# ScalarE's Silu in place of Sigmoid and a VectorE multiply in the attention of a decoder layer

## The reference

```python
qkv = silu(einsum('bnf,of->bno', x, w_qkv))      # 16 heads, 128 wide
q, k, v = split(qkv)
qk = einsum('bhmd,bhnd->bhmn', q, k) * decay      # causal, decays with the distance
out = einsum('bhmn,bhne->bhme', qk, v)            # the block form of the reference sums to this
out = norm_w * (out * rsqrt(mean(out * out) + 1e-6))
gate = sigmoid(einsum('bnf,of->bno', x, w_gate))
result = einsum('bno,fo->bnf', gate * out, w_out)
```

## Time and profile before

| | |
|---|---|
| median of 3 runs | 2632.61 us (2632.53 to 2634.94) |
| the profiled execution, its own time | 2630.53 us |
| its span, first to last instruction | 2628.8 us |
| mean granted clock of TensorE | 0.993 of full speed |
| busy: TensorE, VectorE, ScalarE, GpSimd | 98%, 81%, 42%, 26% of the span |
| ACT_TABLE_LOAD on ScalarE | 92 in the program |

### The profile page before, as it was taken

The page is one execution under the profiler, slowest core; times in us unless marked ns, Lnnn a source line. Parts: engine busy times, 40 slices in busy tenths (PEclk is TensorE's granted clock), DMA queues, the critical chain, the costliest instruction groups (busy, mean ns, idle before and its releaser), DMA issues.

```text
span 2628.8 us, 37692 instructions
## 1 busy us (share of the span) xinstructions
PE 2577.9 (98%) x12735; PEld 2102.3 (80%) x12735; DVE 2130.2 (81%) x4130; ACT 1100.7 (42%) x1862; POOL 690.5 (26%) x1030
## 2 busy tenths in 40 slices
PE   9999999999999999999999999999989999999995
PEld 7888888888888888888888888888877676767762
DVE  8888888887778888777888888777747888888887
ACT  4433333433335444333534443343324555555553
POOL 2111211311122231111223211022223444444444
PEclk9999999999999999999999999999999999999998
DMA  5555455444347654444665544363566555556632
GB/s 217 215 209 189 146 187 192 159 141 129 133 154 235 187 162 160 133 143 139 197 209 187 165 144 129 136 249 144 192 224 181 159 156 167 152 162 168 164 109 56
DMA packets 244943, 439.05 MB, mean 167 GB/s; under 512 B 100240, under 2 KB 135952, under 8 KB 236048
## 3 DMA queue, kind: packets, MB, share of 16 engines
q1 hardware_dynamic: 161056, 407.90, 46.1%
q10 hardware_dynamic: 81360, 20.07, 4.3%
q0 software_dynamic: 2336, 8.65, 1.6%
HBM read 286.35 MB, written 130.17 MB: 158 GB/s over the span
## 4 chain that ended last, share of the span: by engine, by line
PE 93%; DVE 4%; DMA 2%; issue 1%; ACT 1%; POOL 0%; SPq 0%; ACTq 0%; DVEq 0%; POOLq 0%
PE bank L834 39%; PE bank L1529 13%; PE bank L815 13%; PE bank L950 9%; PE bank L904 9%; PE bank L1573 6%; PE bank L1583 3%; PE bank L1550 1%; DMA attention_shared<-attention_x_in 1%; PE bank L1539 1%; DVE attention_stats L1007 0%; DMA finish_qT<-finish_q 0%; PE bank L842 0%; DMA finish_tT<-down_named 0%; PE bank L1561 0%
## 5 line engine op out<-in xcount | busy, mean ns | idle before, releaser
L834 PE MATMUL bank<-attention_xT,attention_w_hi 128*128 128x512 f32 x3064 | 948.4, 391 | 0.0
L834 PEld LDWEIGHTS bank<-attention_xT,attention_w_hi 128*128 128x128 f32 x3064 | 571.3, 188 | 114.5
L834 PE MATMUL bank<-attention_xT,attention_w_lo 128*128 128x512 f32 x1532 | 597.2, 390 | 0.0
L608 POOL TENSOR_TENSOR attention_sq_sum<-attention_sq_sum,attention_sq 128x512 f32<-128x512 f32 x120 | 188.3, 1569 | 966.9 <-ACT attention_sq L777 966.9
L834 PEld LDWEIGHTS bank<-attention_xT,attention_w_lo 128*128 128x128 f32 x1532 | 287.9, 188 | 59.6
L815 PE MATMUL bank<-attention_w_hi,attention_xT 128*128 128x512 f32 x1024 | 325.9, 400 | 9.6 <-DVE attention_sig_v L984 9.4
L734 ACT CAST attention_sh<-attention_sf 128x384 fp32r<-128x384 f32 (+1 forms) x384 | 186.0, 548 | 283.9 <-DVE attention_sf L1133 283.8
L1529 PE MATMUL bank<-finish_w_out_hi,finish_og 128*128 128x512 f32 x824 | 282.8, 408 | 0.2
L1143 DVE TENSOR_TENSOR attention_sl<-attention_sf,attention_sh 128x384 fp32r<-128x384 f32 (+1 forms) x384 | 227.8, 649 | 0.0
L815 PEld LDWEIGHTS bank<-attention_w_hi,attention_xT 128*128 128x128 f32 x1024 | 184.5, 190 | 42.9 <-issue 11.0
L1175 DVE SCALAR_TENSOR_TENSOR attention_og<-bank,attention_nw,attention_gate 128x512 f32<-128x512 f32 x128 | 96.0, 750 | 132.6 <-PE bank L950 119.1
(11 more groups left out here) (225 smaller groups left out, 4921.7 us busy)
## 6 DMA issues: line engine op xcount, KB each, us to landing
attention_xT<-normed_turned SPq DMA_DIRECT2D x62, 2048.0 KB, 8.6
gated_heads<-attention_og_out SPq DMA_DIRECT2D x64, 1024.0 KB, 7.7
finish_og<-gated_heads SPq DMA_DIRECT2D x103, 512.0 KB, 3.9
values<-attention_held SPq DMA_DIRECT2D x128, 256.0 KB, 2.8
attention_vh<-values SPq DMA_DIRECT2D x32, 512.0 KB, 8.1
attention_vl<-values SPq DMA_DIRECT2D x32, 512.0 KB, 9.4
finish_og_last<-gated_heads SPq DMA_DIRECT2D x25, 512.0 KB, 4.0
normed_turned<-attention_shared SPq DMA_DIRECT2D x24, 512.0 KB, 4.1
```

Of the source, the lines that this page charges most:

```text
L608: g.tensor_tensor(sq_sum[:, col_b], sq_sum[:, col_b], sq[:, :], ALU.add).then_inc(s_acc, 1)
L834: mm = pe.matmul(dst[:, :], part[a][w][:, k, col:col + P], xT[i][:, b, k, :], start=(k == 0 and s == 0), stop=(k == KD - 1 and s == 2))
```

## The change

ScalarE writes Silu instead of Sigmoid for queries, keys and values, into buffers with new names. VectorE's multiply by the bank is gone in all three (3 x 128 instructions), so its cast waits for ScalarE directly. The semaphores of steps count one less a round. TensorE's wait before a block of values is now for ScalarE's Silu of the block before, not for VectorE's multiply; so is the wait before the fourth transposition of x. The instruction that has the Sigmoid table loaded ahead of time (L706) now does so for Silu. The gate stays a Sigmoid.

```diff
-            nc.scalar.activation(sig_q[:, :], Q_BANK[:, :], ACT.Sigmoid).then_inc(s_sigq, 1)
+            nc.scalar.activation(silu_q[:, :], Q_BANK[:, :], ACT.Silu).then_inc(s_siluq, 1)
...
-            nc.scalar.activation(sig_k[:, :], K_BANK[:, :], ACT.Sigmoid).then_inc(s_sigk, 1)
+            nc.scalar.activation(silu_k[:, :], K_BANK[:, :], ACT.Silu).then_inc(s_siluk, 1)
...
-            nc.scalar.activation(sig_v[:, :], v_bank(q)[:, :], ACT.Sigmoid).then_inc(s_sigv, 1)
+            nc.scalar.activation(silu_v[:, :], v_bank(q)[:, :], ACT.Silu).then_inc(s_siluv, 1)
...
-        nc.scalar.activation(warm[:, :], dist[:, 0:1], ACT.Sigmoid)
+        nc.scalar.activation(warm[:, :], dist[:, 0:1], ACT.Silu)
...
             if q > 1:
-                pe.wait_ge(s_vm, 2 * (q - 2) + 3 if q > 2 else 1)
+                pe.wait_ge(s_siluv, q if q > 2 else 1)
...
             if n in PREPARED and PREPARED[n] > 1:
-                pe.wait_ge(s_qm, 2 * n + 3)
+                pe.wait_ge(s_siluq, n + 2)
...
-        def silu_split(n, src, f, h, l, sigd, steps, lo):
+        def split(n, f, h, l, sigd, steps, lo):
 
             v_.wait_ge(sigd, n + 1)
-            v_.tensor_tensor(f[:, :], src[:, :], f[:, :], ALU.mult).then_inc(steps, 1)
-            v_.wait_ge(steps, 2 * n + 1)
             v_.tensor_copy(h, f[:, :]).then_inc(steps, 1)
-            v_.wait_ge(steps, 2 * n + 2)
+            v_.wait_ge(steps, n + 1)
             v_.tensor_tensor(l, f[:, :], h.bitcast(F32), ALU.subtract).then_inc(lo, 1)
...
-            v_.wait_ge(s_sigv, q + 1)
-            v_.tensor_tensor(sig_v[:, :], v_bank(q)[:, :], sig_v[:, :], ALU.mult).then_inc(s_vm, 1)
-            v_.wait_ge(s_vm, 2 * q + 1)
+            v_.wait_ge(s_siluv, q + 1)
```

More of the change, by code:

```diff
@@ L225, in attention @@
     og_out = sb("og_out", [P, KT, 2, 2, P])
-    sig_q, sig_k, sig_v = sb("sig_q", [P, S]), sb("sig_k", [P, S]), sb("sig_v", [P, S])
+    silu_q, silu_k, silu_v = sb("silu_q", [P, S]), sb("silu_k", [P, S]), sb("silu_v", [P, S])
     qh, ql = sb("qh", [P, S], F32R), sb("ql", [P, S], F32R)
@@ L717, in scalar @@
         values_hi(1)
-        sig_query(0)
-        sig_key(0)
+        silu_query(0)
+        silu_key(0)
         weights_hi(QK1_W, 0)
-        sig_values(0)
+        silu_values(0)
         weights_hi(G_W, 0)
-        sig_values(1)
+        silu_values(1)
         for n, v, p, b, j in slots():
@@ L745, in scalar @@
             if n < LAST:
-                sig_query(n + 1)
-                sig_key(n + 1)
+                silu_query(n + 1)
+                silu_key(n + 1)
             if b == B - 2 and j == 1 and p + 1 < NP:
@@ L974, in queries @@
                 v_.wait_ge(s_s, 3 * n)
-            silu_split(n, Q_BANK, sig_q, qh[:, :], ql[:, :], s_sigq, s_qm, s_ql)
+            split(n, silu_q, qh[:, :], ql[:, :], s_siluq, s_qm, s_ql)
         def keys(n):
-            silu_split(n, K_BANK, sig_k, kh[:, :], kl[:, :], s_sigk, s_km, s_kl)
+            split(n, silu_k, kh[:, :], kl[:, :], s_siluk, s_km, s_kl)
         def values(q):
             t, i, r = q % KT, q // KT % B % 2, q % 2
-            v_.wait_ge(s_sigv, q + 1)
-            v_.tensor_tensor(sig_v[:, :], v_bank(q)[:, :], sig_v[:, :], ALU.mult).then_inc(s_vm, 1)
-            v_.wait_ge(s_vm, 2 * q + 1)
+            v_.wait_ge(s_siluv, q + 1)
             if q > 1:
@@ L988, in values @@
             own, other = slice(0, 2 * P), slice(2 * P, 4 * P)
-            v_.tensor_copy(vh[i][:, t, :], sig_v[:, own])
-            v_.tensor_copy(held[r][:, 0, :], sig_v[:, other]).then_inc(s_vm, 1)
-            v_.wait_ge(s_vm, 2 * q + 2)
-            v_.tensor_tensor(vl[i][:, t, :], sig_v[:, own], vh[i][:, t, :].bitcast(F32), ALU.subtract)
-            v_.tensor_tensor(held[r][:, 1, :], sig_v[:, other], held[r][:, 0, :].bitcast(F32), ALU.subtract
+            v_.tensor_copy(vh[i][:, t, :], silu_v[:, own])
+            v_.tensor_copy(held[r][:, 0, :], silu_v[:, other]).then_inc(s_vm, 1)
+            v_.wait_ge(s_vm, q + 1)
+            v_.tensor_tensor(vl[i][:, t, :], silu_v[:, own], vh[i][:, t, :].bitcast(F32), ALU.subtract)
+            v_.tensor_tensor(held[r][:, 1, :], silu_v[:, other], held[r][:, 0, :].bitcast(F32), ALU.subtract
                              ).then_inc(s_vl, 1)
```

12 lines of the change are left out of this document (6 added, 6 removed).

## The result

The changed kernel takes 2642.20 us (median of 10 runs, 2639.35 to 2645.31) against 2633.34 us for the kernel before (median of 10 runs): a ratio of 1.0032, interval 1.0023 to 1.0041. The forecast was 2625.3 us, faster. The profiled execution took 2643.36 us, its span is 2641.6 us, the mean granted clock 0.989.

A forecast was written before the change was run, and what follows sets the result against it. TensorE, busy 98% of the span, was taken to bound the kernel. Gains of 9.4 us less 2.1 us for table loads gave 7.3 us off 2632.61, so 2625.3 us, with a range of 2619 to 2634.

The forecast's parts named there:

- To these I add 0.3 for the DMA transposition behind such a Silu, which is issued a little later: Table loads ahead of values where ScalarE is late: 0.3 us for a later transposition, within 2.1 us of total cost.
- 1524.53: ... 0.89 us goes: TensorE's gap at 1524.53 us: the ScalarE side is just in time, so the 0.89 us gap goes.
- 1630.20: ... 0.6 again: Block of values at 1630.20 us, where ScalarE is late: the table load makes TensorE's wait 0.6 us worse.
- the multiply of the keys stands ahead of that work and goes, 0.69 us. Nothing.: Slots with statistics or weight rounding before the gate product: the removed 0.69 us multiply offsets the load, no cost.
- The early gaps: TensorE's gaps at 28.32 and 35.00 us: gains of 1.67 and 1.5 us, plus 1.5 us of low clock.
- 1486.98: TensorE's gap there goes, 2.01 us, and so does the low clock behind it, 1.78 us.
- The gaps at 57 and 78: Values blocks at 55.29 and 77.96 us, where ScalarE is late: the table load makes each gap 0.6 us worse.
- which the prediction had as a rival: Gaps only move (chance 0.27): grown gaps at 58 and 78 us may bring the low clock, about 1.8 us each.
- The loads: 239 more table loads of 1.28 us on ScalarE, 306 us, busy 54% of the span; 2.1 us cost in all.
- The rule of the Trainium skill: A table switch costs 1.28 us plus 1.38 us of drain; by that page the time would be about 2652 us.
- The rival on the slower side: New VectorE and GpSimd meetings (chance 0.08), some 2640 us; or table changes holding ScalarE longer (0.07), 2646 us.
- The 1.5 and 1.78 us of low clock in the sum: Gains from TensorE no longer running at 1.2 GHz after the gaps at 35.00 (1.5 us) and 1486.98 (1.78 us).

The follow-up runs named there:

- e5: Kernel before the change, with VectorE's multiply of the keys left out in slots 97 and 103 only, no table load added; 2645.99 us, ratio 1.0048.
- e6: Changed kernel, with GpSimd loading the 1408-wide weight rows before its wait for the Square, some 9 us ahead of the transposition; 2624.03 us, ratio 0.9961.
- e8: e6 with the gate also a Silu instead of a Sigmoid, so no table is changed in the slots; 2618.03 us, ratio 0.9940.
- e7: Kernel before the change, with the same early load of the 1408-wide weight rows as e6; 2632.82 us, ratio 0.9993.
- e2: Changed kernel, with GpSimd's load of 1408-wide weight rows waiting for VectorE's differences of the block of values, some 2 us later; 2627.52 us, ratio 0.9975.
- e9: Changed kernel, with one extra VectorE instruction of 0.69 us ahead of the keys' split in slots 97 and 103; 2638.81 us, ratio 1.0016.
- e11: e9 plus the edit of e1: the store of gated heads also waits for the Silu of the values; 2625.03 us, ratio 0.9957.
- e3: Kernel before the change, with the 1408-wide transposition issued after VectorE's multiply of the values, 1.20 us behind the store, rows' load held back; 2631.96 us, ratio 0.9991.
- e12: e2 with the load of rows waiting for VectorE's casts instead of the differences, 0.8 us earlier; 2634.51 us, ratio 0.9999.
- e1: Changed kernel, with SyncE's store of gated heads in slots 97 and 103 waiting for the Silu of the values, behind the transposition; 2640.59 us, ratio 1.0023.

## Why the prediction was wrong, point by point

- **The step that failed** is in the costs of the loads: "To these I add 0.3 for the DMA transposition behind such a Silu, which is issued a little later", and with it "1524.53: ... 0.89 us goes" and "1630.20: ... 0.6 again". It priced the transposition as a fixed thing that starts later. It starts no later against TensorE; its neighbours start earlier, and it then takes 19 us instead of 13. I credited 0.89 and charged 0.6 + 0.3; the two places cost 13.2 us of gaps and 4.0 of low clock in the profile.
- **A sign of it was there to be read.** The chain of waits of the kernel before holds, between blocks of values:

```profile
1607.31 2.80 PE bank L815 x12
1610.14 14.81 DMA attention_shared<-attention_x_in
1630.20 3.00 PE bank L815 x12
```

  The transposition of slot 103 was already on the chain, 14.81 us long, with L698 waiting 1.44 us for it. I read the 0.81 us gap as ScalarE's Square being late and did not ask what the Square was late for. Its length should have been a term with a range of its own. The same holds for "1524.53: the ScalarE side is just in time": it is, but the gap came from VectorE's two slow instructions, and these from the load of rows that landed late.
- **The same multiply was counted for nothing in the wrong place.** The prediction says that where rounding of weights stands between the keys and the gate product "the multiply of the keys stands ahead of that work and goes, 0.69 us. Nothing." On the engines that is right. It did not follow the DMAs that this 0.69 us starts earlier; e5 shows that it alone costs 12 us in two slots (interval of the ratio 1.0035 to 1.0062, that is 9 to 16 us).
- **The early gaps**: right. 28.32 and 35.00 are gone with their low clock; the gate product of slot 0 stands 4.9 us earlier in e6 than before, where 1.67 + 1.5 + 1.5 = 4.7 was forecast. 1486.98 is gone with its clock too: from slot 95 to slot 98 the lead grows by 3.5 us (1.45 to 4.98), against 3.79.
- **The gaps at 57 and 78**: 1.64 and 1.85, as the 1.6 and 1.85 of the sum. But the second brought the low clock, which the prediction had as a rival: the lead of 4.9 falls to 2.1 and 2.9 us in slots 2 and 3, some 2.4 us against the 1.2 forecast.
- **The loads**: 1283 ns each, 239 more, ScalarE at 54%: right. TensorE waits in no ordinary slot, since the 16.7 us are four gaps. Their price without the meeting is 5 to 6 us (e8), not 2.1: a mis-sized term.
- **The rule of the Trainium skill** ("ScalarE: Activation LUTs", "What ACT_TABLE_LOAD costs") would put 1.38 us of drain on each switch. By the rows, the load starts 0.01 us behind the end of the Square (1497.78), ends at 1499.07, and the Silu starts at 1499.09; no run here shows the drain. That the time came out slower does not bear the rule out: with every load in place e6 is faster than before.
- **The rival on the slower side** named new meetings of VectorE and GpSimd, in dozens of slots, and a longer change of table. The loss came from two slots and a DMA; neither described it.
- The whole, without the meeting: 8.8 us between e7 and e6 against the forecast 7.3, and 2624.0 against 2625.3. These agree partly by luck: more gained than summed, and more paid for the loads. The 1.5 and 1.78 us of low clock in the sum are luck of another kind: they were read from one execution, and the profiled one of e7 has the same gaps (1.66, 1.82 and 2.01) with the clock at 1.00 behind them.

**What stays open**: what inside the DMA engines makes the transposition's packets 2.5 times as long. The runs show that the load of rows and the store close by each count. They don't show by which queue or buffer, nor whether the 2 MB load of `attention_xT` must be under way: in slots 100 and 106 the transpositions land in 3.5 to 6.1 us, even with the load of rows at +0.55 (slot 100 of the changed kernel, 5.6), but there neither `attention_xT` nor the 1 MB store is near, and no run takes out one of the two alone.

## What to carry to other kernels

A faster engine that is "off the path" still starts transfers: for each stretch where it runs without idle time, list the DMAs issued behind it and their distance to the other issues near them, before and after. Look in the chain of waits for a DMA whose time has no slack, even if the wait it makes is only a microsecond: its length is not a constant. And when a change of this kind loses, try moving the one transfer before giving the change up: here that turned 0.3% slower into 0.4% faster.

## What was new about the chip

- A DMA transposition (1440 packets, 0.36 MB) landed in anything from 7.5 to 20.7 us in slots 97 and 103, by when its neighbours were issued, with a load of 2 MB issued shortly ahead of it; its share of the engines' time over 35 us went from 5.2% to 17.1%. The Trainium skill ("DMA: Bandwidth & Descriptors", "Issuing engines are not separate DMA queues") says that issuing from several engines saves little but the time on the sequencers; three issuing engines were at work here, and by e2, e6 and the pair e9 and e11 their transfers do hold each other up. In the changed kernel the load of rows beside it suffered as well, 18.9 us against 4.5 in e6.
- Once the transposition is issued in 2.2 us and once in 5.4 on ScalarE's queue. In slot 97 the issues of 3.4 us and more go with a store ahead or at +0.09 (after, e2, e3, e6, e9, e12), those of 2.2 to 2.3 with a store at +0.21 or later (before, e1, e7, e11), but a short issue did not mean an early landing (e1).
- The same gap of TensorE brings the 1.2 GHz level in one execution and not in another. Gaps of 1.82 and 2.01 us did so in the kernel before (PEclk 0.57 from 36 to 40 us, 0.50 from 1487 to 1490) and one of 1.85 in the changed kernel. In e7 those of 1.82 and 2.01, and in e2 those of 1.85 and 2.12, left the clock at full speed:

```profile
36.00:40.00 4.00, 4.00 (x19) 3.30 (x18) 4.00 (x10) 2.77 (x6) 0.00 (x0) 1.00 0.19 66
1489.00:1493.00 4.00, 4.00 (x20) 3.29 (x19) 4.00 (x10) 2.83 (x5) 0.00 (x0) 1.00 0.20 68
...
74.00:80.00 6.00, 6.00 (x28) 4.94 (x28) 5.87 (x15) 3.70 (x7) 0.46 (x1) 1.00 1.03 330
1624.00:1629.00 5.00, 5.00 (x23) 4.13 (x22) 4.97 (x13) 1.95 (x4) 0.00 (x0) 1.00 0.15 52
```

  (The first two are e7, the last two e2.) The gaps of 1.00, 1.24 and 1.64 us in the kernels before and after brought no low clock, and each one of 2.28 us (e12) and above before L815 in slots 98 and 104 did.
